# Scan layer of a four-layer network on one core: softplus by ScalarE's own function, three of sixteen products on GpSimd, x added by TensorE, rows issued by SyncE

## The chip, the core and the metric

The kernel runs on one core of a Trainium2 chip. The time is that of one execution on the device, in microseconds. The median of three runs of the kernel before was 3129.49 us (3125.74 to 3132.32). Five engines work side by side, each through its own list of instructions in the written order: TensorE (PE in the profile, its weight loads PEld), VectorE (DVE), ScalarE (ACT), GpSimd (POOL) and SyncE (SP), which here only issues DMAs. They wait for each other through semaphores. SBUF is the working memory of 128 partitions; PSUM is the one TensorE writes to.

## What is computed

Three triangle layers come first and aren't touched. The fourth is a selective scan (Mamba) over the image: 256 columns, each a sequence of 256 rows with 32 channels, group-normalised first, and added to x at the end.

```python
xz = xs @ W_in; xi, z = jnp.split(xz, 2, axis=-1)            # 64 + 64
xc = silu(causal_conv(xi, conv_w) + conv_b)                   # 4 taps
dt_r, Bc, Cc = jnp.split(xc @ W_x, [dtr, dtr + d_state], -1)  # 2, 16, 16
dt = softplus(dt_r @ W_dt + b_dt)
A = -jnp.exp(A_log)
def step(h, inp):
    x_t, dt_t, B_t, C_t = inp
    h = jnp.exp(dt_t[:, :, None] * A) * h + dt_t[:, :, None] * B_t[:, None, :] * x_t[:, :, None]
    return (h, jnp.einsum('bds,bs->bd', h, C_t))
y = (scan(step, h0, ...) + xc * D_skip) * silu(z)
x = x + y @ W_out
```

All arithmetic is float32.

## The kernel before

`mamba_layer` cuts the 256 columns into four groups of 64 that lie on different partitions, and each group into 32 chunks of two columns (SUB). A chunk thus holds eight sequences of 256 rows; they are processed as two halves q of four sequences each along the 1024 free elements (W; HALF is 512) and 64 channels on two blocks of partitions. A state tile has 16 states x 8 channels on its 128 partitions, so a chunk has 16 **steps** s: eight groups of channels (dg) for each half q. In a step:

- SP loads the rows of dt for this group from DRAM, spread over the states, into `dtb` (ring of 4, 512 KB, L541).
- ACT makes the decays exp(dt*A) from `dtb` into `da` (ring of 4, L399). It does so one step ahead: in step s it makes those of s+1.
- PE spreads dt*x over the states into the PSUM tile `pb[s % 2]` (L282), waiting until scan s-2 has released it.
- DVE multiplies `pb` by B in place (L472), then scans with `da` and `pb` into `hs` (ring of 4, L477).
- POOL multiplies `hs` by C (L500).
- PE sums over the states into `py` (L265), for step s-3 (LAG). At dg 0 it starts the sum with D_skip*x (L261).

Beside its steps each engine has shares of the preparation of the next chunk (PRE), of its own chunk (OWN), of the one after next (NEXT2) and of the chunk before (POST). The table `SHARES` gives for each engine the step after which a share stands; function `schedule` writes step, shares, next step, share... in that order for each engine. Nothing moves later: this written order is what each engine follows. The shares: xg (normalised input, ACT L321), x (convolution, PE L230, four matmuls, silu L334), z (PE L236, silu L343), dt (PE L241, softplus on ACT and POOL), bq and cq (B and C of a half, PE L249, copied by ACT L391), take (y from PSUM, ACT L309), gate (times silu z, POOL L506), out (PE L293), its sum with x into `fin` (DVE L484), the stores of fin (ACT L416) and the rows of dt to DRAM (ACT L357). The softplus is built as max(v, 0) + ln(1 + exp(-|v|)) with a correction of the rounding of 1 + u: six ACT operations of full width (L364 to L383) and, on POOL, six operations of half width (L517, L520, L524), then dt*x in two halves (L527).

x, dt, z, bq and cq pass through the same two PSUM banks `misc[0..1]`. The table `USE` fixes their turn in a chunk; each writer on PE waits until ACT has emptied the bank of the one before. Before, that turn is x, bq1, cq1, dt, z, bq0, cq0. The chunks 1 to 28 run in a hardware loop of 14 rounds of two.

Of the kernel before, what the change touches and what calls it, by code (L numbers as in the profile page):

```python
# [5 lines left out]
P = 128  # L6
# [3 lines left out]
ALU = mybir.AluOpType  # L10
# [3 lines left out]
def mamba_layer(nc, shared, dt_dram, out):  # L14
# [15 lines left out]
    LAG = 3  # L30

    with ExitStack() as ctx:
# [11 lines left out]
        minus_one = sb("minus_one", [P, 1])  # L44
# [5 lines left out]
        (avg, w_in, conv_w, w_z, wx_dt, w_dt, w_bc, w_out, w_skip, vecs, a_log, spread, gather) = (t for t, _ in shared.weights)  # L50
# [16 lines left out]
        hs = sb("hs", [P, H_RING, W])  # L67
        gated = sb("gated", [P, W])
# [12 lines left out]
        with nc.Block() as block:  # L81
# [23 lines left out]
            def _(v):  # L105
                nc.vector.memset(minus_one[:, :], -1.0)
# [34 lines left out]
        def early(k, n):  # L141
            return isinstance(k, int) and k < n

        FIRST_USE = {"x": 0, "dt": 1, "z": 2, "bq0": 3, "cq0": 4}
        USE = {"x": 0, "bq1": 1, "cq1": 2, "dt": 3, "z": 4, "bq0": 5, "cq0": 6}

        def use(k, name):
            if early(k, 1) and name in FIRST_USE:
                return FIRST_USE[name]
            body = k if name in ("bq1", "cq1") else k - 1  # L150
            if isinstance(k, int) and body == CHUNKS - 1:
                return len(FIRST_USE) + len(USE) * body + ("bq1", "cq1").index(name)
            return len(FIRST_USE) + len(USE) * body + USE[name]

        def stores_of(k, par):
# [62 lines left out]
        with nc.Block() as block:  # L218
            @block.tensor
            def _(pe):  # L220
                def pre(k, par, op):
# [47 lines left out]
                def steps(k, par, s, first, last):  # L269
# [1365 lines left out]
```

## Time and profile before

| | |
|---|---|
| median of three runs | 3129.49 us |
| span of the profiled execution | 3123.6 us |
| scan layer, first scan to end of last | 1295.6 to 3110.6 us |
| busy over the whole span: PE, DVE, ACT, POOL | 82%, 80%, 61%, 66% |

The profile is of one execution. Its busy shares over the whole span mix the triangle layers (until about 1240 us) with the scan layer; for the change the rows of the second half count. Rows of a timeline give start and duration in us, the engine, the line of the kernel, the operation, output and inputs with their sizes, the count of merged instructions and, in brackets, the idle time of the engine before them with what ended it. A matmul in float32 leaves two records, so x8 stands for four matmuls.

### The profile page before, as it was taken

To read this page: it belongs to the slowest core of one execution; us is meant where nothing else is said; L and a number is where in the kernel's file an instruction comes from. 1 tells how busy PE (TensorE), PEld (TensorE's weight loads), DVE (VectorE), ACT (ScalarE), POOL (GpSimd) and SP (SyncE) were. 2 spreads that over 40 slices of the span, in tenths; PEclk is the share of its full clock that TensorE was granted. 3 is DMA by queue.
4 is the path that set the end of the run, shared out by engine and by line. 5 is a ranking of instruction groups with operands and counts; after the bars stand their busy time and mean duration, and the time that the engine had idled before them with its cause. 6 is when DMAs were issued, how large, how long until landed. Compare 5 with 4: busy or idle time off the path is not lost.

```text
span 3123.6 us, 40760 instructions
## 1 busy us (share of the span) xinstructions
PE 2573.1 (82%) x12954; PEld 756.1 (24%) x12954; DVE 2485.6 (80%) x2176; ACT 1914.4 (61%) x2402; POOL 2065.3 (66%) x1284
## 2 busy tenths in 40 slices
PE   5888878888788775688888888888888888888886
PEld 1233123331233211222222222222222222222221
DVE  5655656555555544599999999999999999999998
ACT  4534654346543343667777777677777776777772
POOL 2543245432444313298898888988988889889886
PEclk9999999999999988799999999999999999999999
DMA  4797327863279647667677677676775766767765
GB/s 162 241 325 212 102 67 255 294 205 102 72 241 313 192 133 181 132 146 181 147 165 167 144 177 163 148 181 148 162 170 145 179 160 148 180 148 162 171 145 117
DMA packets 257701, 537.53 MB, mean 172 GB/s; under 512 B 39608, under 2 KB 150656, under 8 KB 256688
## 3 DMA queue, kind: packets, MB, share of 16 engines
q1 hardware_dynamic: 215328, 444.01, 53.7%
q0 software_dynamic: 19040, 64.24, 7.7%
q10 hardware_dynamic: 23216, 27.74, 3.7%
q8 instruction: 71, 1.16, 0.2%
q14 instruction: 46, 0.38, 0.0%
HBM read 396.55 MB, written 139.33 MB: 172 GB/s over the span
## 4 chain that ended last, share of the span: by engine, by line
POOL 29%; issue 27%; PE 5%; DVE 2%; DMA 2%; ACT 1%; SPq 1%; POOLq 0%; ACTq 0%; DVEq 0%
POOL m_hs L500 18%; POOL m_sp_v L517 2%; POOL m_dtx L527 2%; POOL m_gated L506 2%; DMA t_tile<-band_out 1%; POOL m_dt L524 1%; POOL m_dt L520 1%; SPq L913 1%; DVE m_pb L472 1%; PE t_bank L1096 1%; PE t_bank L1057 1%; PE t_bank L1021 1%; POOL t_xc L1481 1%; DVE m_hs L477 1%; PE m_misc L230 0%
## 5 line engine op out<-in xcount | busy, mean ns | idle before, releaser
L500 POOL TENSOR_TENSOR m_hs<-m_hs,m_cs 128x1024 f32<-128x1024 f32 x512 | 1203.6, 2358 | 288.4 <-DVE m_hs L477 288.4
L477 DVE TENSOR_TENSOR_SCAN m_hs<-m_da,m_pb 128x1024 f32<-128x1024 f32 x512 | 1170.7, 2287 | 29.3 <-ACT m_da L399 4.2
L399 ACT ACTIVATE m_da<-m_dtb,m_a_neg 128x1020 f32<-128x1020 f32 x512 | 576.6, 1144 | 275.9 <-DMA m_dtb<-dt_rows 254.1
L282 PE MATMUL m_pb<-m_dtx,late 64*128 64x512 f32 x2048 | 583.5, 646 | 150.2 <-DVE m_hs L477 146.9
L265 PE MATMUL m_py<-m_hs,late 128*64 128x512 f32 x2048 | 565.8, 631 | 104.8 <-POOL m_hs L500 104.0
L472 DVE TENSOR_TENSOR m_pb<-m_pb,m_bs 128x1024 f32<-128x1024 f32 x512 | 619.7, 1210 | 20.9 <-PE m_pb L282 20.9
L1481 POOL TENSOR_TENSOR t_xc<-t_xc,big 128x512 f32<-128x512 f32 x96 | 120.1, 1271 | 338.8 <-DVE big L1387 338.8
L282 PEld LDWEIGHTS m_pb<-m_dtx,late 64*128 64x128 f32 x2048 | 163.4, 188 | 567.3 <-DVE m_hs L477 457.5
L1021 PE MATMUL t_bank<-late,t_lwin 128*128 128x256 f32 x816 | 217.3, 404 | 63.3 <-ACT big L1260 34.0
L1359 DVE SCALAR_TENSOR_TENSOR t_xc<-t_bank,t_vec,t_xc 128x512 f32<-128x512 f32 x96 | 72.0, 750 | 244.2 <-PE t_bank L1057 244.2
L1248 ACT ACTIVATE t_sq<-t_bank 128x512 f32<-128x512 f32 x192 | 105.5, 598 | 245.3 <-PE t_bank L1096 245.2
L1257 ACT ACTIVATE t_gate<-t_bank,t_small 128x512 f32<-128x512 f32 x192 | 121.4, 683 | 191.0 <-PE t_bank L1031 190.9
L265 PEld LDWEIGHTS m_py<-m_hs,late 128*64 128x64 f32 x2048 | 102.5, 136 | 509.3 <-POOL m_hs L500 279.6
L1478 POOL TENSOR_TENSOR t_sq<-big 128x512 f32<-128x512 f32 x96 | 103.1, 1082 | 185.2 <-ACT big L1230 112.2
L1377 DVE SCALAR_TENSOR_TENSOR t_tile<-t_bank,t_small,t_gate 128x512 f32<-128x512 f32 x192 | 135.2, 746 | 89.6 <-issue 59.4
L1344 DVE TENSOR_TENSOR t_vwin<-t_bank,t_mask_k 128x512 f32<-128x512 f32 x204 | 138.0, 687 | 83.9 <-PE t_bank L1021 64.8
L1413 POOL DMA_DIRECT2D late<-right_factor x96 | 56.9, 593 | 212.6 <-PE t_bank L1021 156.4
L1021 PEld LDWEIGHTS t_bank<-late,t_lwin 128*128 128x128 f32 x816 | 146.6, 193 | 175.3 <-issue 83.3
L1096 PE MATMUL t_bank<-t_tile,t_center 64*64 64x512 f32 x768 | 125.8, 668 | 68.8 <-DMA t_tile<-band_out 54.6
L391 ACT COPY m_cs<-m_misc 128x512 f32<-128x512 f32 x128 | 68.7, 589 | 154.1 <-PE m_misc L249 154.1
L321 ACT ACTIVATE m_xg<-big,m_gn_bias,m_gn_scale 64x512 f32 (+1 forms) x126 | 161.2, 1279 | 1.7
L249 PE MATMUL m_misc<-m_act,late 64*128 64x512 f32 x512 | 147.1, 651 | 13.6 <-ACT m_act L343 11.1
(166 smaller groups left out, 3591.3 us busy)
## 6 DMA issues: line engine op xcount, KB each, us to landing
m_dtb<-dt_rows SPq DMA_DIRECT2D x512, 512.0 KB, 6.1
late<-right_factor POOLq DMA_DIRECT2D x102, 512.0 KB, 5.5
right_factor<-t_tile SPq DMA_DIRECT2D x192, 256.0 KB, 3.5
t_tile<-band_out SPq DMA_DIRECT2D x183, 256.0 KB, 4.2
band_out<-t_vwin SPq DMA_DIRECT2D x48, 512.0 KB
band_out<-t_vwin SPq DMA_DIRECT2D x48, 480.0 KB
dt_rows<-m_dt ACTq DMA_DIRECT2D x64, 256.0 KB, 3.2
t_xc<-in_x_cm SPq DMA_DIRECT2D x4, 2048.0 KB, 14.6
```

What stands on the lines that cost most here:

```text
L249: nc.tensor.matmul(misc[n][:, :], w_bc[rows, b, :], act[par][rows, half(q)], start=True, stop=True).then_inc(misc_ready[n], 1)
L265: m = nc.tensor.matmul(py[q][D * n:D * n + D, :], gather[:, dg, :], hs[:, s % H_RING, half(n)], start=False, stop=(dg == DG - 1), skip_gro ...
L282: m = nc.tensor.matmul(pb[s % 2][:, half(n)], spread[rows, dg, :], dtx[par][rows, half(q)], start=True, stop=True)
L321: m = nc.scalar.activation(xg[par][P // 4 * shift:P // 4 * shift + P // 2, q, :, first:first + T], xm[rows, :, bass.ds(SUB * k, SUB)].rear ...
L399: nc.scalar.activation(da[:, s % DA_RING, :, 1:T], dtb[s % DTB_RING][:, :].rearrange("p (r t) -> p r t", t=T)[:, :, 1:T], ACT.Exp, scale=a ...
L472: nc.vector.tensor_tensor(pb[s % 2][:, :], pb[s % 2][:, :], bs[q][:, :], ALU.mult).then_inc(u_done, 1)
L477: nc.vector.tensor_tensor_scan(hs[:, s % H_RING, :], da[:, s % DA_RING, :, :].rearrange("p r t -> p (r t)"), pb[s % 2][:, :], 0.0, ALU.mul ...
L500: nc.gpsimd.tensor_tensor(hs[:, s % H_RING, :], hs[:, s % H_RING, :], cs[q][:, :], ALU.mult).then_inc(hc_ready, 1)
L1021: m = nc.tensor.matmul(bank[b][:, e * COLS:(e + 1) * COLS], lwin[:, slot, LROW * h + BAND:LROW * h + BAND + P], rwin[:, slot, h * COLS:(h ...
L1096: m = nc.tensor.matmul(bank[p][o:o + HID, :], center64[HID * hs:HID * hs + HID, HID * hs:HID * hs + HID], tile[HID * hs:HID * hs + HID, sl ...
L1344: nc.vector.tensor_tensor(vwin[:, slot, UNIT * j:UNIT * j + UNIT].rearrange("p (h k) -> p h k", k=COLS), bank[b][:, :].rearrange("p (h k) ...
L1481: nc.gpsimd.tensor_tensor(x_unit(n), x_unit(n), xn_unit(n), ALU.add).then_inc(x_done, 1)
```

## The change

- **Softplus.** One ACT activation per half (Softplus with bias) from `misc` to `dt`. The six ACT operations and the six on POOL are gone. Silus of x and z stand together at step 6; the table is loaded for silu, back, for softplus at step 8, back.
- **Products.** For s in POOL_U (5, 10, 15) PE spreads dt*x into `misc` instead of `pb` (shares u5, u10, u15, at steps 0, 4, 10), ACT copies it to `ub` (ring of 2), POOL multiplies it by B. The decays of these steps go to the PSUM tile `pb[s % 2]`, which has no product in that step. ACT first writes the zeros of its first columns, and waits for scan s-2 instead of s-4.
- **Turn of misc.** u5, bq1, cq1, u10, x, z, dt, bq0, u15, cq0. On PE x and z both stand after step 5.
- **x** is added by a matmul of an identity (`eye`, a new weight) with x, read with a step of a row, into py[1] ahead of out; ACT copies the sum to `fin` at step 9.
- **SP** issues the rows of dt (step 13) and the stores of fin (step 14).
- The loop of 14 rounds is written out.

```diff
+    POOL_U = (5, 10, 15)
+    UB_RING = 2
...
-        USE = {"x": 0, "bq1": 1, "cq1": 2, "dt": 3, "z": 4, "bq0": 5, "cq0": 6}
+        FIRST_USE = {op: i for i, op in enumerate(("x", "z", "dt", "bq0", "cq0"))}
+        USE = {op: i for i, op in enumerate(("u5", "bq1", "cq1", "u10", "x", "z", "dt", "bq0", "u15", "cq0"))}
...
-            "tensor": {0: [(PRE, "x")], 2: [(OWN, "bq1")], 4: [(OWN, "cq1")], 5: [(PRE, "dt")],
-                       8: [(PRE, "z"), (POST, "out")], 9: [(PRE, "bq0")], 11: [(PRE, "cq0")]},
...
+            "tensor": {0: [(OWN, "u5")], 1: [(OWN, "bq1")], 3: [(OWN, "cq1")], 4: [(OWN, "u10")], 5: [(PRE, "x"), (PRE, "z")],
+                       7: [(PRE, "dt")], 8: [(POST, "out")], 9: [(PRE, "bq0")], 10: [(OWN, "u15")], 11: [(PRE, "cq0")]},
+            "scalar": {1: [(OWN, "u5")], 2: [(OWN, "bq1")], 4: [(POST, "take1"), (OWN, "cq1")], 5: [(OWN, "u10")], 6: [(PRE, "silu")],
+                       8: [(PRE, "dt")], 9: [(POST, "fin")], 10: [(PRE, "bq0")], 11: [(OWN, "u15")], 12: [(PRE, "cq0"), (OWN, "take0")],
+                       13: [(NEXT2, "xg0")], 15: [(NEXT2, "xg1")]},
+            "vector": {},
+            "gpsimd": {1: [(OWN, "u5")], 5: [(POST, "gate1")], 6: [(OWN, "u10")], 9: [(PRE, "dtx0")], 10: [(PRE, "dtx1")], 11: [(OWN, "u15")],
+                       13: [(OWN, "gate0")]},
+            "sync": {13: [(PRE, "dt_rows")], 14: [(POST, "store")]},
...
-            with eng.Fori(1, CHUNKS - 4, 2) as k:
-                chunk(k, 1, (NEXT2, PRE, OWN, POST))
-                chunk(k + 1, 0, (NEXT2, PRE, OWN, POST))
-            chunk(CHUNKS - 3, 1, (NEXT2, PRE, OWN, POST))
+            for k in range(1, CHUNKS - 2):
+                chunk(k, k % 2, (NEXT2, PRE, OWN, POST))
...
+                    elif op[0] == "u":
+                        q, dg = divmod(int(op[1:]), DG)
+                        pe.wait_ge(dtx_ready, 2 * k + q + 1)
+                        for n in range(2):
+                            pe.wait_ge(misc_used[n], use(k, op))
+                        for n in range(2):
+                            rows = slice(D * n, D * n + D)
+                            nc.tensor.matmul(misc[n][:, :], spread[rows, dg, :], dtx[par][rows, half(q)],
+                                             start=True, stop=True).then_inc(misc_ready[n], 1)
...
-                    if not (first and s < 2):
-                        pe.wait_ge(h_ready, g - 1)
...
+                    if s not in POOL_U:
+                        if not (first and s < 2):
+                            pe.wait_ge(h_ready, g - 1)
...
+                    nc.tensor.matmul(py[1][:, :], eye[:, :], xm[:, :, SUB * k:SUB * k + SUB].rearrange("p t n -> p n t"),
+                                     start=True, stop=False, skip_group_check=True)
...
+                    elif op == "dt":
+                        a.preload_act_table_set("softplus")
...
+                            nc.scalar.activation(dt[:, half(q)], misc[q][:, :], ACT.Softplus, bias=b_dt).then_inc(misc_used[q], 1)
+                        a.preload_act_table_set("natural_log_exp_and_others")
...
+                    if s in POOL_U:
+                        a.wait_ge(h_ready, g - 1)
+                        to = pb[s % 2][:, :].rearrange("p (r t) -> p r t", t=T)
+                        nc.scalar.copy(to[:, :, 0:1], zeros[:, :].unsqueeze(2))
+                    else:
+                        if not (first and s < DA_RING):
+                            a.wait_ge(h_ready, g - DA_RING + 1)
+                        to = da[:, s % DA_RING, :, :]
+                    nc.scalar.activation(to[:, :, 1:T], rows, ACT.Exp, scale=a_neg[:, dg:dg + 1]).then_inc(da_ready, 1)
...
+                    a.wait_ge(o_ready, k + 1)
+                    if not early(k, 1):
+                        a.wait_ge(stored, 16 * G * k)
+                    nc.scalar.copy(fin[:, :], py[1][:, :]).then_inc(fin_done, 1)
...
+                    decays, products = da[:, s % DA_RING, :, :].rearrange("p r t -> p (r t)"), pb[s % 2][:, :]
+                    if s in POOL_U:
+                        j = pool_products(k, s)
+                        v.wait_ge(ub_ready, j + 1)
+                        decays, products = pb[s % 2][:, :], ub[j % UB_RING][:, :]
```

## Rows read from the trace of the kernel before

**Rows 1.** The page, part 1: busy us, share of the span, instructions.
```profile
PE 2573.1 (82%) x12954; PEld 756.1 (24%) x12954; DVE 2485.6 (80%) x2176; ACT 1914.4 (61%) x2402; POOL 2065.3 (66%) x1284
```

**Rows 2.** First to last scan: length; busy PE, PEld, DVE, ACT, POOL; clock; DMA share; GB/s.
```profile
1295.60:3110.60 1815.00, 1558.73 (x5334) 410.89 (x5332) 1778.87 (x1054) 1317.53 (x1442) 1577.46 (x822) 0.99 0.69 160
```

**Rows 3.** Groups by line, 1400 to 3110 us: busy us, mean ns | idle before, releaser.
```profile
L500 POOL TENSOR_TENSOR m_hs<-m_hs,m_cs 128x1024 f32<-128x1024 f32 x483 | 1135.3, 2358 | 214.9 <-DVE m_hs L477 214.9
L477 DVE TENSOR_TENSOR_SCAN m_hs<-m_da,m_pb 128x1024 f32<-128x1024 f32 x483 | 1104.4, 2287 | 23.8
L472 DVE TENSOR_TENSOR m_pb<-m_pb,m_bs 128x1024 f32<-128x1024 f32 x482 | 583.4, 1210 | 10.0 <-PE m_pb L282 10.0
...
L321 ACT ACTIVATE m_xg<-big,m_gn_bias,m_gn_scale 64x512 f32 x110 | 140.7, 1279 | 1.5
...
L520 POOL TENSOR_TENSOR m_dt<-m_dt,m_sp_v 128x512 f32<-128x512 f32 x58 | 74.2, 1279 | 2.3
...
L334 ACT ACTIVATE m_act<-m_misc,late 128x512 f32<-128x512 f32 x58 | 36.7, 684 | 0.3
...
L484 DVE TENSOR_TENSOR m_fin<-m_py,big 128x512 f32<-128x512 f32 x30 | 31.2, 1039 | 0.0
L364 ACT ACTIVATE m_sp_u<-m_sp_x 128x1024 f32<-128x1024 f32 x29 | 30.7, 1057 | 2.3
```

**Rows 4.** Waits of DVE, 1400 to 3100 us: us in total, times, longest us.
```profile
DVE m_pb L472 <- PE m_pb L282: 10.0, 29, 0.6
```

**Rows 5.** Timeline of DVE in one chunk.
```profile
2263.31 1.23 DVE L472 TENSOR_TENSOR m_pb<-m_pb,m_bs 128x1024 f32<-128x1024 f32 x1 [0.48 <-PE m_pb L282]
...
2278.54 2.29 DVE L477 TENSOR_TENSOR_SCAN m_hs<-m_da,m_pb 128x1024 f32<-128x1024 f32 x1
2280.74 1.21 DVE L472 TENSOR_TENSOR m_pb<-m_pb,m_bs 128x1024 f32<-128x1024 f32 x1
2281.98 2.29 DVE L477 TENSOR_TENSOR_SCAN m_hs<-m_da,m_pb 128x1024 f32<-128x1024 f32 x1
```

**Rows 6.** Timeline of PE in the same chunk.
```profile
2258.21 3.99 PE L230 MATMUL m_misc<-m_xg,m_w_conv 128*128 128x512 f32 x8
2262.14 1.13 PE L282 MATMUL m_pb<-m_dtx,late 64*128 64x512 f32 x4
2263.20 1.08 PE L265 MATMUL m_py<-m_hs,late 128*64 128x512 f32 x4
...
2286.39 1.98 PE L236 MATMUL m_misc<-m_xg,late 64*128 64x512 f32 x4
2288.30 1.08 PE L293 MATMUL m_py<-m_gated,late 128*64 128x512 f32 x4
```

**Rows 7.** Timeline of ACT in the same chunk.
```profile
2262.39 1.28 ACT L328 ACT_TABLE_LOAD   x1
...
2268.36 1.05 ACT L391 COPY m_bs<-m_misc 128x512 f32<-128x512 f32 x2
2269.30 1.15 ACT L399 ACTIVATE m_da<-m_dtb,m_a_neg 128x1020 f32<-128x1020 f32 x1
2270.34 0.58 ACT L309 COPY m_gated<-m_py 128x512 f32<-128x512 f32 x1
```

**Rows 8.** Groups by line of ACT, whole program: a tiny operation.
```profile
L91 ACT ACTIVATE m_gn_scale<-m_gn_scale 128x1 f32<-128x1 f32 x1 | 0.2, 203 | 0.0
```

**Rows 9.** Timeline of PE at the end of the chunk.
```profile
2302.53 1.13 PE L282 MATMUL m_pb<-m_dtx,late 64*128 64x512 f32 x4 [1.31 <-DVE m_hs L477]
2304.77 1.98 PE L265 MATMUL m_py<-m_hs,late 128*64 128x512 f32 x4 [1.11 <-POOL m_hs L500]
```

**Rows 10.** Stretches of 2 us, columns as in Rows 2: chunk before, this chunk.
```profile
2246.00:2248.00 2.00, 0.88 (x6) 0.18 (x4) 1.97 (x2) 1.97 (x2) 2.00 (x2) 1.00 0.41 98
...
2309.00:2311.00 2.00, 2.00 (x6) 0.42 (x4) 1.97 (x3) 0.00 (x0) 2.00 (x2) 0.51 0.57 176
```

**Rows 11.** Timeline: the first scan.
```profile
1295.61 2.29 DVE L477 TENSOR_TENSOR_SCAN m_hs<-m_da,m_pb 128x1024 f32<-128x1024 f32 x1 [4.21 <-ACT m_da L399]
```

More of the change, by code:

```diff
@@ L67, in mamba_layer @@
         hs = sb("hs", [P, H_RING, W])
+        ub = [sb(f"ub{i}", [P, W]) for i in range(UB_RING)]
+        zeros = sb("zeros", [P, 2 * SUB])
         gated = sb("gated", [P, W])
@@ L141, in early @@
         def early(k, n):
-            return isinstance(k, int) and k < n
-        FIRST_USE = {"x": 0, "dt": 1, "z": 2, "bq0": 3, "cq0": 4}
-        USE = {"x": 0, "bq1": 1, "cq1": 2, "dt": 3, "z": 4, "bq0": 5, "cq0": 6}
+            return k < n
+        FIRST_USE = {op: i for i, op in enumerate(("x", "z", "dt", "bq0", "cq0"))}
+        USE = {op: i for i, op in enumerate(("u5", "bq1", "cq1", "u10", "x", "z", "dt", "bq0", "u15", "cq0"))}
+        OWN_USE = ("u5", "bq1", "cq1", "u10", "u15")
         def use(k, name):
@@ L149, in use, with dve_products, pool_products @@
                 return FIRST_USE[name]
-            body = k if name in ("bq1", "cq1") else k - 1
-            if isinstance(k, int) and body == CHUNKS - 1:
-                return len(FIRST_USE) + len(USE) * body + ("bq1", "cq1").index(name)
+            body = k if name in OWN_USE else k - 1
+            if body == CHUNKS - 1:
+                return len(FIRST_USE) + len(USE) * body + OWN_USE.index(name)
             return len(FIRST_USE) + len(USE) * body + USE[name]
+        def dve_products(k, s):
+            return (S - len(POOL_U)) * k + s - sum(t < s for t in POOL_U)
+        def pool_products(k, s):
+            return len(POOL_U) * k + sum(t < s for t in POOL_U)
         def stores_of(k, par):
@@ L180, in schedule @@
-        def schedule(eng, name, pre, steps, post):
+        FIRST = {"vector": {9: [(PRE, "dtx0"), (PRE, "dtx1")]}, "gpsimd": {}}
+        def schedule(name, pre, steps, post):
             def share(k, par, kinds, s):
-                table = FIRST if kinds == (PRE,) and k == -1 and name in FIRST else FIRST_X if isinstance(k, int) and k == -2 and name in FIRST_X else SHARES
+                table = FIRST if kinds == (PRE,) and k == -1 and name in FIRST else FIRST_X if k == -2 and name in FIRST_X else SHARES
@@ L413, in post @@
                         return take(k, par, 1)
-                    a.wait_ge(fin_done, k + 1)
-                    for g in range(G):
-                        a.dma_start(out[:, bass.ds(SUB * k + g * NG, SUB), :],
-                                    fin[DM * g:DM * g + DM, :].rearrange("p (n t) -> p n t", n=SUB)).then_inc(stored, 16)
-                schedule(a, "scalar", pre, steps, post)
+                    a.wait_ge(o_ready, k + 1)
+                    if not early(k, 1):
+                        a.wait_ge(stored, 16 * G * k)
+                    nc.scalar.copy(fin[:, :], py[1][:, :]).then_inc(fin_done, 1)
+                schedule("scalar", pre, steps, post)
             @block.vector
@@ L476, in steps @@
                         v.wait_ge(hc_used, g - H_RING + 1)
[L477 to L489 removed]
+                    nc.vector.tensor_tensor_scan(hs[:, s % H_RING, :], decays, products, 0.0, ALU.mult, ALU.add).then_inc(h_ready, 1)
+                schedule("vector", pre, steps, None)
             @block.gpsimd
@@ L537, in steps @@
                         sp.wait_ge(dt_stored[par], stores_of(k, par))
-                    elif not (first and s < DTB_RING):
+                    if not (first and s < DTB_RING):
                         sp.wait_ge(da_ready, g - DTB_RING + 1)
@@ L543, in steps, with pre, post @@
                                  ).then_inc(dtb_loaded[s % DTB_RING], 16)
-                schedule(sp, "sync", None, steps, None)
+                def pre(k, par, op):
+                    for q in range(2):
+                        sp.wait_ge(misc_used[q], use(k, "dt") + 1)
+                    if not early(k, 2):
+                        sp.wait_ge(da_ready, S * (k - 1))
+                    for n in range(2):
+                        sp.dma_start(dt_dram[par, :, :, n, :].rearrange("q d c -> d q c"),
+                                     dt[D * n:D * n + D, :].rearrange("d (q c) -> d q c", q=2)).then_inc(dt_stored[par], 16)
+                def post(k, par, op):
+                    sp.wait_ge(fin_done, k + 1)
+                    for g in range(G):
+                        sp.dma_start(out[:, SUB * k + g * NG:SUB * k + g * NG + SUB, :],
+                                     fin[DM * g:DM * g + DM, :].rearrange("p (n t) -> p n t", n=SUB)).then_inc(stored, 16)
+                schedule("sync", pre, steps, post)
                 sp.wait_ge(stored, 16 * G * CHUNKS)
```

201 lines of the change are left out of this document (57 added, 144 removed).

## Prediction

> **What bounds the kernel now.** Read the page's busy shares first [rows 1]: over the whole program no engine is full, but the scan layer is the second half, and there the stretch view is the one to read. Between the first and the last scan, 1815 us, DVE is busy 1778.9 us, 98%, PE 86%, POOL 87%, ACT 73% [rows 2]. That is 32 chunks of 56.7 us. The groups by line say what DVE does in a chunk [rows 3]: 16 scans of 2.29 us and 16 products (L472) of 1.21 us, 56.0 us, and one addition of x (L484) of 1.04 us; neighbours overlap by some 0.05 to 0.09 us. DVE's waits hold one line, the product L472 waiting for PE, 10.0 us in 30 chunks [rows 4]. The timelines show where that is: step to step is 3.45 us [rows 5], except once a chunk, 0.5 us late, because the next matmul of L282 stands in PE's queue behind the x matmuls (3.9 us) [rows 5, 6]. So DVE is the bound, but PE, which works in the written order, has only that much room behind it.
>
> **Work removed and added, per chunk.** On DVE three of 16 products go, and the addition of x. A step whose product comes from elsewhere is a scan alone: 2.2 us from start to start, the distance from a scan to what follows it [rows 5]. 13 x 3.45 + 3 x 2.2 = 51.4 us against 56.7. The scan still reads one operand from PSUM and one from SBUF, only exchanged, so I keep 2.29 us (nothing in the trace has the exchanged form; it could be 0.1 us either way, 0.3 a chunk).
> On POOL six half-width operations of the softplus go (6 x 1.28 = 7.7 us), three products of full width come (3 x 2.36 = 7.1) [rows 3]: 87% of 56.7 is 49.3, now 48.7 us. It fits under 51.4, barely. The products are due three to four steps after they are issued, so POOL delays nothing.
> On ACT six full-width operations of some 1.06 us go [rows 3]; six copies of 0.58, the copy of fin (0.6) and three zero columns (a tiny ACT operation takes 0.20 us [rows 8]) come: 41.2 - 6.4 + 4.7 = 39.5 us. The table loads stay four (before: two pairs around the silus; now silu, exp, softplus, exp) at 1.28 us each [rows 7]. Hidden, as long as ACT is not on a chain; below it is.
> On PE the three spread matmuls only change their target; the identity matmul for x is new. A 128-row matmul of 512 columns takes 1.0 us (a quarter of the 3.9 for x, half of the 1.9 for z [rows 6]). Its moving operand is read with a step of a whole row. The nearest rows for such a read are ACT's L321 at 1.28 us against L334 at 0.68 for a contiguous one [rows 3], a factor of 1.9; so I take 1.9 us, bounds 1.0 and 2.5 (both records of the matmul at 1.28). PE needs about 50 us of a chunk: it too only just fits under 51.4.
> The Trainium skill (SBUF — State Buffer, Door 1) says that SBUF is read in lines of 16 bytes and that each access in a new line pays; that speaks against this matmul. It agrees in direction with L321; by the page alone no figure follows, and with contiguous reads the sum would be unchanged, since the 0.6 us of lateness this gives to product 9 lies beside another one (below).
> The rows of dt leave on SP instead of ACT, at step 13, behind load 13 and ahead of load 14. They no longer wait for POOL's fix-up; SP's loads of the next chunk come earlier. The four stores of fin go to SP too, behind load 14; what queues behind them is loads 15 and on, which run four decays ahead. ACT's long waits for these loads cost DVE nothing before, so I price the move at 0 (bounds -0.5 and +0.5 us a chunk, a load issued late by the 0.6 us or so of each of the six issues).
> The loop of 14 rounds is written out. DVE shows no wait at its ends [rows 4], so nothing is gained there: 0.
>
> **What the new order does.** misc[0..1] now has ten users a chunk in strict turn: u5, bq1, cq1, u10, x, z, dt, bq0, u15, cq0. In PE's written order z has moved up beside x, so between the spread matmul of step 4 and that of step 6 stand: sums 1 and 2, u10, x and z. Step 5 has no spread matmul of its own, so DVE asks for that of step 6 a scan earlier than the pace of the steps suggests. Count from the end of scan 3, t=0. DVE's own path: product 4 at -0.1, scan 4 at 1.15, scan 5 at 3.35, product 6 due at 5.55.
> The supply: the decay of step 5 is written to the PSUM bank that scan 3 read, so ACT waits there until t=0, and the take of y and the copies of cq1 stand behind it on ACT. u10 may write misc only after those copies; PE, in order, waits with everything behind it. Zero column 0.2, decay 1.05, take 0.5, copies 1.1 [rows 7, 8], with 0.1 for the wait: 2.9. u10 1.05 (as the spread matmul L282), sum 2 1.0 [rows 6]: 5.0. x 3.9: 8.9. z 1.9: 10.8 (the silus of x end at 8.3 and 9.7, in time for it, table load included). Spread matmul 6 to product 6 1.2 [rows 5, 6]: **12.0**. Product 6 is 6.5 us late in every chunk that prepares a next one. Even with no wait at all for ACT, PE has 7.0 us between these two matmuls and is given about 9.1 of work, so over 2 us would remain.
> A second, smaller chain of the same kind: decay 10 waits for scan 8; behind it fin 0.5, decay 11 1.05, copies of bq0 1.1, u15 1.1, spread matmul 11 1.2: product 11 starts 6.3 after scan 8 instead of 5.55, 0.7 late. The lateness of product 9 from the identity matmul lies inside it.
> **The clock.** PE idles before u10, from about t=-1.3 (sum 1 done) to 2.9. What a gap does to it is in the trace: at the end of a chunk, after idle times of 1.3 and 1.1 us around one matmul group, the granted clock fell from 1.00 to 0.50 (1.2 GHz) until about 2311, the sums then taking 1.97 us instead of 1.08; in the chunk before, the same pattern passed at 1.00 [rows 9, 10]. A gap of 4.2 us is larger than these, so I expect the half clock under u10 and the first x matmuls in nearly all chunks. The Trainium skill (TensorE: Matmul & The Clock Gate, What's actually happening) says that the low clock is the default and activity lifts it; the row agrees. Rows show low stretches that cost from 0 up to 3.1 us (half of 6.2); I take 1.7, about the middle. Near the chunk's end two more gaps (waits for POOL at sum 12 and for scan 14) can do the same; the matmuls there have about a step of room, so 0.5 (0 to 1.5).
>
> **The sum.** Chunk: 51.4 + 6.5 + 0.7 + 1.7 + 0.5 = 60.8 us against 56.7, +4.1. Thirty-one chunks prepare a next one: +127. The last has no x and z: 51.4 + 0.7, -4.6. Ahead of the first scan (1295.6 [rows 11]) the softplus chain of three ACT and nine DVE pieces goes and z comes in: -6 (-8 to 0). At the end fin is 0.4 shorter, the identity matmul adds up to 2 at the low clock: +1.5. Together +118. Profiled execution 3123.6 -> 3242; the median of the runs stands 5.9 higher, 3129.5 -> **3247 us**. Low end: clock terms 0, chain 0.5 shorter: 58.1 a chunk, 31 x 1.4 - 9 = +34, 3163. High end: 3.1 + 1.5 for the clock, 0.6 more for the identity matmul: 63.8, 31 x 7.1 - 9 = +211, about 3340.
>
> **The rivals.**
> A. *DVE stays the bound*: no lateness at products 6 and 11, 51.9 us a chunk with small waits: -154 -5, about 2970, clearly faster. For it: each engine's work fits, POOL and PE under 51.4. Against: it needs spread matmul 6 to start by t=4.4, that is x and z out of the way before; with DVE's pace given, PE would have to take later matmuls first. What decides is PE's order. That it keeps it the trace shows: the spread matmul at 2262.14 stood ready behind x while DVE waited [rows 5, 6]. The Trainium skill (TensorE: Matmul & The Clock Gate, Step-by-step: what each phase is for) says that matmuls stay in program order and only weight loads are pulled ahead; by that rule this rival falls.
> B. *Only PE's load counts*: ACT frees misc earlier than I hold (the wait for scan 3 ends early), product 6 about 2.6 late: 51.4 + 2.6 + 0.7, -2.0 a chunk, about 3060. Against: the wait is written ahead of the copies on ACT, and nothing lets ACT pass it.
> C. *The strided matmul is dear*, 4 us rather than 1.9: product 9 becomes 2.7 late, +2.0 on each chunk on top of the forecast: about 3310.
> D. *The added and the saved cancel*: chain 3 us shorter and the clock held: within 0.2%.
>
> **How the numbers follow.** Forecast (lateness at product 6 of 5 us or more) 0.69; C 0.08; A 0.13; B 0.07; D 0.03. Slower 0.77, same 0.03, faster 0.20 (0.2%, 6 us, is about what can be told from no change). The range has to reach from the forecast's low end, with something for a shorter chain, to C: 3145 to 3335; A and B stay out of it.
>
> **What would show it.** Timeline of DVE: product 6 starts some 12 us after scan 3 ends, not 5.6, and DVE's waits name PE at L472 with about 200 us or more; DVE's share falls from 98% to about 85%. Timeline of PE: idle before u10 until the copies of cq1, then x and z back to back, the clock near 0.5 at its start. ACT idle before decay 5 until scan 3. If product 6 is in time, the chain is wrong; if the x matmuls run at 1.00, the clock term is; if the identity matmul takes 1.0 us, its price was too high, with no effect on the sum.

## The result and the profile after

The changed kernel takes 3252.55 us, the median of 4 runs (3238.95 to 3266.88), against 3129.97 (3125.74 to 3132.32, also 4) for the kernel before on the same chip: ratio 1.0385, interval 1.0345 to 1.0425. It is slower by 3.9%. The profiled execution spans 3242.0 us, against 3123.6.

First the page: busy time, and the slices of DVE and of PE's clock.

```profile
PE 2700.6 (83%) x13018; PEld 808.9 (25%) x13018; DVE 2342.8 (72%) x2039; ACT 1859.9 (57%) x2534; POOL 2053.0 (63%) x1194
...
DVE  5655656556554442878888888888888889788787
...
PEclk9999999999989887899899998999998999898998
```

In [rows 1] DVE was busy 80% of the span; now it has 143 us less work and the span is 118 us longer. In the scan layer no engine is full any more. This is the stretch 1400 to 3000 us (columns as in [rows 2]); DVE is at 85%, where [rows 2] had 98%:

```profile
1400.00:3000.00 1600.00, 1398.66 (x4518) 384.93 (x4514) 1365.97 (x772) 1065.03 (x1322) 1306.03 (x613) 0.92 0.61 153
```

The waits from 1400 to 3220 us name what DVE, PE and ACT stand still for (total, times, longest). This answers [rows 4], where DVE waited 10.0 us in all:

```profile
DVE m_pb L450 <- PE m_pb L290: 255.1, 137, 9.0
...
PE m_misc L243 <- ACT m_cs L380: 104.2, 30, 3.7
PE m_py L272 <- POOL m_hs L468: 77.7, 30, 2.6
...
ACT m_pb L390 <- DVE m_hs L455: 388.4, 90, 10.0
```

L450 is now DVE's product, L455 the scan, L290 the spread matmul, L243 the matmul of a product for POOL, L272 the sum over states, L468 POOL's product with C, L380 the copies of B and C, L390 the zero column ahead of a decay in PSUM. The first, second and last of these lines, read upwards, make a circle: ACT waits for a scan, PE for ACT's copies, DVE for PE.

One chunk as DVE sees it (the place of [rows 5]): scans 3, 4 and 5, then product 6 after 5.89 us of idling, and products 9 and 12.

```profile
2334.35 2.29 DVE L455 TENSOR_TENSOR_SCAN m_hs<-m_da,m_pb 128x1024 f32<-128x1024 f32 x1
...
2337.80 2.29 DVE L455 TENSOR_TENSOR_SCAN m_hs<-m_da,m_pb 128x1024 f32<-128x1024 f32 x1
2340.00 2.27 DVE L455 TENSOR_TENSOR_SCAN m_hs<-m_pb,m_ub 128x1024 f32<-128x1024 f32 x1
2348.16 1.23 DVE L450 TENSOR_TENSOR m_pb<-m_pb,m_bs 128x1024 f32<-128x1024 f32 x1 [5.89 <-PE m_pb L290]
...
2359.18 1.23 DVE L450 TENSOR_TENSOR m_pb<-m_pb,m_bs 128x1024 f32<-128x1024 f32 x1 [0.57 <-PE m_pb L290]
...
2368.58 1.23 DVE L450 TENSOR_TENSOR m_pb<-m_pb,m_bs 128x1024 f32<-128x1024 f32 x1 [0.23 <-PE m_pb L290]
```

The same microseconds on ACT and PE (the places of [rows 7] and [rows 6]):

```profile
2336.73 0.17 ACT L390 COPY m_pb<-m_zeros 128x4 f32<-128x4 f32 x1 [6.29 <-DVE m_hs L455]
2336.83 1.11 ACT L395 ACTIVATE m_pb<-m_dtb,m_a_neg 128x1020 f32<-128x1020 f32 x1
2337.88 0.58 ACT L319 COPY m_gated<-m_py 128x512 f32<-128x512 f32 x1
2338.36 1.07 ACT L380 COPY m_cs<-m_misc 128x512 f32<-128x512 f32 x2
```

```profile
2339.57 1.13 PE L243 MATMUL m_misc<-m_dtx,late 64*128 64x512 f32 x4 [3.43 <-ACT m_cs L380]
2340.63 1.08 PE L272 MATMUL m_py<-m_hs,late 128*64 128x512 f32 x4
2341.64 3.70 PE L228 MATMUL m_misc<-m_xg,m_w_conv 128*128 128x512 f32 x8
2345.27 1.55 PE L234 MATMUL m_misc<-m_xg,late 64*128 64x512 f32 x3
...
2346.77 1.33 PE L290 MATMUL m_pb<-m_dtx,late 64*128 64x512 f32 x3
...
2355.10 1.96 PE L300 MATMUL m_py<-big,late 128*128 128x512 f32 x2
```

Scan 3 ends at 2336.64, and ACT's zero column starts 0.09 us later. Decay, take and copies run to 2339.43, u10, sum 2, x and z to 2347.25, the first of the four spread matmuls of step 6 among those of z. Product 6 starts 11.5 us after the scan. Here the clock was at 1.00 throughout. In other chunks it fell: PE was idle from 2394.7 to 2398.2, then sum 2 took 1.85 us instead of 1.08 and x 4.58 instead of 3.70. Stretches of 2 us, clock in the third column from the right:

```profile
2398.00:2400.00 2.00, 1.80 (x6) 0.53 (x8) 2.00 (x2) 1.71 (x4) 1.20 (x1) 0.86 0.92 219
2400.00:2402.00 2.00, 2.00 (x5) 0.50 (x2) 0.90 (x1) 1.98 (x3) 2.00 (x2) 0.50 0.90 225
2402.00:2404.00 2.00, 2.00 (x5) 0.90 (x4) 0.00 (x0) 0.81 (x1) 2.00 (x2) 0.79 0.86 174
```

### The profile page after: what moved, and what is told of

It reads as the page before. It is cut to its first block, busy times and chain, and to the rows that moved or that the text cites. A ratio compares the mean times of both kernels' runs of the same rounds, so it can differ in the third digit from the quotient of the medians.

```text
span 3242.0 us, 37780 instructions
## 1 busy us (share of the span) xinstructions
PE 2700.6 (83%) x13018; PEld 808.9 (25%) x13018; DVE 2342.8 (72%) x2039; ACT 1859.9 (57%) x2534; POOL 2053.0 (63%) x1194
## 3 DMA queue, kind: packets, MB, share of 16 engines
q1 hardware_dynamic: 230832, 469.25, 52.1%
## 4 chain that ended last, share of the span: by engine, by line
DVE 23%; PE 21%; issue 11%; ACT 5%; POOL 1%; DVEq 0%; ACTq 0%; POOLq 0%
DVE m_hs L455 12%; DVE m_pb L450 11%; PE m_pb L290 5%; PE m_misc L228 4%; PE m_py L272 4%; PE m_misc L243 3%; PE m_misc L234 2%; PE m_misc L256 1%; PE m_py L268 1%; ACT m_bs L380 1%; ACT m_cs L380 1%; ACT m_da L395 1%; ACT m_gated L319 1%; ACT m_fin L411 1%; POOL m_hs L468 0%
## 5 line engine op out<-in xcount | busy, mean ns | idle before, releaser
L468 POOL TENSOR_TENSOR m_hs<-m_hs,m_cs 128x1024 f32<-128x1024 f32 x512 | 1199.2, 2353 | 414.2 <-DVE m_hs L455 410.9
L455 DVE TENSOR_TENSOR_SCAN m_hs<-m_da,m_pb 128x1024 f32<-128x1024 f32 x416 | 951.2, 2286 | 19.3 <-ACT m_da L395 4.9
L450 DVE TENSOR_TENSOR m_pb<-m_pb,m_bs 128x1024 f32<-128x1024 f32 x416 | 505.8, 1216 | 279.4 <-PE m_pb L290 279.4
L272 PE MATMUL m_py<-m_hs,late 128*64 128x512 f32 x2048 | 613.1, 680 | 85.2 <-POOL m_hs L468 85.2
L290 PE MATMUL m_pb<-m_dtx,late 64*128 64x512 f32 x1664 | 509.3, 660 | 42.8 <-DVE m_hs L455 42.8
L395 ACT ACTIVATE m_da<-m_dtb,m_a_neg 128x1020 f32<-128x1020 f32 x416 | 472.2, 1150 | 2.1
L390 ACT COPY m_pb<-m_zeros 128x4 f32<-128x4 f32 x96 | 15.8, 165 | 419.8 <-DVE m_hs L455 419.8
L290 PEld LDWEIGHTS m_pb<-m_dtx,late 64*128 64x128 f32 x1664 | 161.3, 197 | 332.3 <-issue 249.0
L272 PEld LDWEIGHTS m_py<-m_hs,late 128*64 128x64 f32 x2048 | 107.5, 143 | 511.1 <-issue 311.1
L243 PE MATMUL m_misc<-m_dtx,late 64*128 64x512 f32 x384 | 125.0, 726 | 124.5 <-ACT m_cs L380 111.1
L484 POOL TENSOR_TENSOR m_ub<-m_ub,m_bs 128x1024 f32<-128x1024 f32 x96 | 226.1, 2356 | 0.0
L455 DVE TENSOR_TENSOR_SCAN m_hs<-m_pb,m_ub 128x1024 f32<-128x1024 f32 x96 | 217.3, 2264 | 0.0
```

What stands on the lines that cost most here:

```text
L243: nc.tensor.matmul(misc[n][:, :], spread[rows, dg, :], dtx[par][rows, half(q)], start=True, stop=True).then_inc(misc_ready[n], 1)
L272: m = nc.tensor.matmul(py[q][D * n:D * n + D, :], gather[:, dg, :], hs[:, s % H_RING, half(n)], start=False, stop=(dg == DG - 1), skip_gro ...
L290: m = nc.tensor.matmul(pb[s % 2][:, half(n)], spread[rows, dg, :], dtx[par][rows, half(q)], start=True, stop=True)
L395: nc.scalar.activation(to[:, :, 1:T], rows, ACT.Exp, scale=a_neg[:, dg:dg + 1]).then_inc(da_ready, 1)
L450: nc.vector.tensor_tensor(products, products, bs[q][:, :], ALU.mult).then_inc(u_done, 1)
L455: nc.vector.tensor_tensor_scan(hs[:, s % H_RING, :], decays, products, 0.0, ALU.mult, ALU.add).then_inc(h_ready, 1)
```

## The experiments

Times are medians; ratios are to the kernel before on the same chip. A chunk is the distance between the first scans of neighbouring chunks, its mean over the 31 chunks that have a next one (from the timelines of DVE). It belongs to the one execution that was profiled; for "z a step later" that was the slowest of the four (3259.5 us, the others 3226.3 to 3233.6), so its 61.2 is too long for the median beside it. The kernels ran on several chips, so the ratios compare better than the medians.

| kernel | us | ratio, interval | chunk, us |
|---|---|---|---|
| before | 3129.97 | | 56.8 |
| after | 3252.55 | 1.0385, 1.0345 to 1.0425 | 60.5 |
| z a step later | 3230.6 | 1.0315, 1.0266 to 1.0365 | 61.2 |
| decays in SBUF | 3159.9 | 1.0066, 1.0034 to 1.0098 | 57.9 |
| copies ahead of the pinned decay | 3120.6 | 0.9953, 0.9931 to 0.9975 | 56.7 |
| PE's gap filled | 3199.1 | 1.0199, 1.0170 to 1.0227 | 59.2 |
| x read contiguously | 3233.7 | 1.0306, 1.0276 to 1.0337 | 60.5 |
| no products on POOL | 3163.3 | 1.0066, 1.0029 to 1.0102 | 57.7 |
| the same, z at step 7 | 3145.7 | 1.0030, 1.0015 to 1.0045 | 57.5 |
| the same, steps 7 to 10 spread | 3107.8 | 0.9917, 0.9896 to 0.9939 | 56.3 |
| PE reordered, x on DVE | 3052.3 | 0.9732, 0.9704 to 0.9759 | 54.5 |
| PE reordered, x on PE | 3053.3 | 0.9732, 0.9716 to 0.9749 | 54.5 |
| reordered, clock kept, x on DVE | 2987.2 | 0.9516, 0.9496 to 0.9536 | 52.4 |
| reordered, clock kept, x on PE | 2977.5 | 0.9506, 0.9482 to 0.9529 | 52.1 |

**Is it z alone?**

```
-  5: [(PRE, "x"), (PRE, "z")],
+  5: [(PRE, "x")], 6: [(PRE, "z")],
```

> The changed kernel with z moved on PE from behind x (step 5) to behind step 6; all else stays. Theory (PE works through a block without a pause from u10 to the spread matmul of step 9, so only the total in that block and the pause ahead of it count): the wait of product 6 falls by 1.9 us, from 5.9 to 8.4 down to about 4 to 6.5, products 7 to 9 become late instead (about 0.5, 0.5 and 1.5 us), and the time stays within 0.3% of the changed kernel, 3240 to 3260 us. Rival (the place of z at step 5 is what costs): 31 x 1.9 = 59 us less, about 3190 us.

Waits of DVE in one chunk:

```profile
2237.99 1.23 DVE L450 TENSOR_TENSOR m_pb<-m_pb,m_bs 128x1024 f32<-128x1024 f32 x1 [7.22 <-PE m_pb L290]
2241.77 1.23 DVE L450 TENSOR_TENSOR m_pb<-m_pb,m_bs 128x1024 f32<-128x1024 f32 x1 [0.23 <-PE m_pb L290]
2245.85 1.23 DVE L450 TENSOR_TENSOR m_pb<-m_pb,m_bs 128x1024 f32<-128x1024 f32 x1 [0.52 <-PE m_pb L290]
2250.72 1.23 DVE L450 TENSOR_TENSOR m_pb<-m_pb,m_bs 128x1024 f32<-128x1024 f32 x1 [1.32 <-PE m_pb L290]
```

Product 6 still waits 5.6 to 7.4 us, and what z gave back is asked for again at products 7 to 9. PE was late as a whole; taking one block out of one gap only passes the lateness on. The time is that of after or up to 1% less, 3230.6 us where 3240 to 3260 was expected; the rival asked for 3190.

**Is it the pinned decay?** First without it: the decays of 5, 10 and 15 go to the SBUF ring like the others.

```
-  if s in POOL_U:
-      a.wait_ge(h_ready, g - 1)
-      to = pb[s % 2][:, :].rearrange("p (r t) -> p r t", t=T)
-      nc.scalar.copy(to[:, :, 0:1], zeros[:, :].unsqueeze(2))
-  else:
   if not (first and s < DA_RING):
       a.wait_ge(h_ready, g - DA_RING + 1)
   to = da[:, s % DA_RING, :, :]
...
-  decays, products = pb[s % 2][:, :], ub[j % UB_RING][:, :]
+  products = ub[j % UB_RING][:, :]
```

> The changed kernel with the decays of steps 5, 10 and 15 in the SBUF ring like all others, waiting for the scan four steps back; no zero columns. Theory (the pin of ACT on the scan two steps back, ahead of the copies of cq1, delays u10): ACT copies cq1 early, product 6 waits about 2.6 us instead of 5.9 to 8.4, PE has no long pause before u10 and keeps its clock: 55 us a chunk instead of 60.3, about 3090 us. Rival 1 (ACT is not the cause, only the amount of work on PE): product 6 waits 6 us or more and the time stays near 3250. Rival 2 (a scan with both operands in SBUF is slower, by POOL's use of SBUF for instance): mean of these 96 scans above 2.35 us.

The wait of product 6 fell to 3.12 us (2.6 expected):

```profile
2303.97 1.23 DVE L445 TENSOR_TENSOR m_pb<-m_pb,m_bs 128x1024 f32<-128x1024 f32 x1 [3.12 <-PE m_pb L290]
```

The theory of the pin holds, but the time missed, 3159.9 us where 3090 was expected, and the chunk fell only to 57.9. Here rival 2 came true as well: the 91 scans with both operands in SBUF took 2.92 us on average (1400 to 3150 us) where 2.35 was its mark, since they collide with POOL. At three such scans a chunk that is 1.9 us. Scans and POOL's operations of one stretch:

```profile
2318.74 2.27 DVE L450 TENSOR_TENSOR_SCAN m_hs<-m_da,m_ub 128x1024 f32<-128x1024 f32 x1
...
2335.17 4.18 DVE L450 TENSOR_TENSOR_SCAN m_hs<-m_da,m_ub 128x1024 f32<-128x1024 f32 x1
```

```profile
2318.90 4.26 POOL L463 TENSOR_TENSOR m_hs<-m_hs,m_cs 128x1024 f32<-128x1024 f32 x1 [1.95 <-DVE m_hs L450]
...
2332.55 4.66 POOL L463 TENSOR_TENSOR m_hs<-m_hs,m_cs 128x1024 f32<-128x1024 f32 x2
2337.17 3.24 POOL L469 TENSOR_TENSOR m_gated<-m_gated,m_act 128x512 f32<-128x512 f32 x1
```

The scan that began first (2318.74) took its 2.27 us, and POOL's operation, begun 0.16 later, 4.26 instead of 2.35: 1.91 longer, where 2.1 of the scan were left. The scan at 2335.17 met a running POOL operation that ended at 2337.21 and took 4.18; the gate that began then took 3.24 instead of 1.27. Each waits out the other whole. In after, with one operand in PSUM, no scan is long: 91 with a mean of 2.264 us. The Trainium skill (SBUF — State Buffer, Who interferes with whom) says that a VectorE instruction with two inputs in SBUF and a GpSimd one that reads SBUF exclude each other for a whole instruction, and that the first to start wins; these rows agree, with the four durations above. So placing those decays in PSUM has a purpose: it costs ACT the pin and saves the scans this.

Then with the pin, but the copies no longer behind it:

```
 tensor  -  3: cq1, 4: u10, 5: x, z         +  2: cq1, 3: u10, 5: x, z
 scalar  -  4: take1, cq1, 5: u10           +  3: cq1, u10, 4: take1
```

> The changed kernel with cq1 and u10 each a step earlier on PE and both copied ahead of the pinned decay 5 on ACT; decays in PSUM, x and z behind step 5 as in the changed kernel. Theory (the pin is in the chain, and what is left is the amount of work between two spread matmuls): product 6 waits about 2.6 us instead of 5.9 to 8.4, no low clock in front of x: 55.1 us a chunk, about 3085 us. Rival 1 (the pin doesn't matter): product 6 still 6 us or more late, 3240 us. Rival 2 (x and z together don't matter once the pin is out of the way): under 1 us, about 3040 us.

```profile
2221.79 1.55 PE L234 MATMUL m_misc<-m_xg,late 64*128 64x512 f32 x3 [1.02 <-ACT m_act L343]
```

Product 6 waits 3.21 us in nearly every chunk instead of 5.89 to 8.40 (the row below), PE no longer idles before u10, and 132 us are gone (3252.6 to 3120.6): slower has become slightly faster. The run moves two things together: the copies ahead of the pin, and u10, 1.0 us, out of the block between spread matmuls 4 and 6. What each brings, and what comes from the clock, isn't separated by it; the run before moves the pin alone, but pays with long scans. The time is 35 us more than expected: x now ends so early that z waits 1.02 for the silu of x (the line above), and product 1 waits 0.76 to 1.38 us in 18 of the 31 chunks behind the pauses at the chunk's end, with matmuls at twice their time there.

```profile
2224.68 1.23 DVE L450 TENSOR_TENSOR m_pb<-m_pb,m_bs 128x1024 f32<-128x1024 f32 x1 [3.21 <-PE m_pb L290]
```

**Is the clock a cost of its own?** Three matmuls with zero weights (zw), added to a bank already being summed, before u10:

```
+  if op == "u10":
+      for _ in range(3):
+          nc.tensor.matmul(py[0][:, :], zw[:, :], act[par][:, half(0)], start=False, stop=False,
+                           skip_group_check=True)
```

> The changed kernel with three matmuls of a zero weight (128 rows, 512 columns, adding nothing) on PE ahead of the wait of u10: 3 us of work more per chunk in a pause of about 4.2 us. Theory (the pause lowers the granted clock in two chunks of three): waits of product 6 all near 5.9 us instead of 5.9, 7.5, 8.4, the time 31 x 1.4 = 43 us less, about 3210 us. Rival (the three values come from something else, DMA for instance): no gain, or up to 30 us more for the work added, 3250 to 3280 us.

With work added, the time fell by 53 us (43 expected). Product 6 waits 5.89 to 6.17 in all chunks that prepare a next one, but for the first (5.40), and the mean clock rose from 0.924 to 0.942. The mean of its three waits in after is (5.89 + 7.54 + 8.40) / 3 = 7.28 us, so the clock cost about 1.4 us a chunk there; the chunks agree, 60.5 against 59.2.

**The strided read.** Here other elements of x are added, read contiguously:

```
-  xm[:, :, SUB * k:SUB * k + SUB].rearrange("p t n -> p n t")
+  shared.big[:, HALF * k:HALF * k + HALF]
```

> The changed kernel with the identity matmul reading 512 elements in a row instead of 512 with a step of a row; it adds other elements of x than the reference. Theory: the matmul takes 1.0 us instead of 1.96; the 0.6 us of wait at product 9 goes and comes back at product 11 through the chain decay 10, fin, decay 11, bq0, u15; the time stays within 0.3% of the changed kernel, 3240 to 3260 us. Rival (each us of PE counts one for one): 31 x 0.9 = 28 us less, about 3225 us.

Groups of after and of this kernel:

```profile
L300 PE MATMUL m_py<-big,late 128*128 128x512 f32 x60 | 58.8, 1069 | 0.0
```

```profile
L300 PE MATMUL m_py<-big,late 128*128 128x512 f32 x60 | 33.8, 645 | 0.0
```

The stride costs 0.42 us on each of two records. Product 9's wait of 0.57 went, 0.35 came at product 11 and product 12 waited 0.44 instead of 0.23, and the chunk stayed at 60.5: no term of the sum. The median is 19 us lower all the same, a little below the 3240 expected; of the 10.7 us between the two profiled spans 8.0 lie ahead of the first scan and 2.5 in the chunks.

**Softplus, fin and SP alone.** `POOL_U = ()`, and u5, u10, u15 out of all tables (a); then z moved (b); then the blocks spread, fin at step 10 with them (c). PE's steps:

```
 (a)  5: x, z   7: dt    8: out         9: bq0
 (b)  5: x      7: z     8: dt, out     9: bq0
 (c)  5: x      7: z     8: dt          9: out        10: bq0
```

> The changed kernel with all 16 products on DVE and all decays in SBUF; softplus, fin by identity matmul, SP's rows and the order with x and z behind step 5 stay. Theory (x and z back to back, 5.8 us between two spread matmuls, are late even without a pinned decay): product 6 waits about 2.3 us, a chunk takes 55.2 + 2.3 + 0.5 = 58 us, about 3165 us. Rival (the pin alone makes the lateness): product 6 waits 0.5 us or less, 55.7 us a chunk, 3090 us.

> As e7_no_products, with z behind step 7 and dt behind step 8. Theory: no wait of DVE over 0.6 us, 55.6 us a chunk, so what the softplus, fin on PE and SP's rows bring by themselves: 32 x 1.1 + 6, about 3090 us. Rival (the new parts have a cost of their own besides the order): 3120 us or more.

> As e8_no_products_z7, with out and the identity matmul a step later (9), bq0 behind step 10 and fin on ACT at step 10, so that no block of over 3 us but x stands between two spread matmuls. Theory (e8's wait of 2.1 us a chunk came from dt, identity and out standing together behind step 8): waits of DVE under 0.6 us a chunk, 55.8 us a chunk, 3129.5 - 32 x 0.9 - 6 = about 3095 us, the gain of softplus and fin without the products. Rival (something else in the new parts costs): 3130 us or more.

Waits of DVE in (a), (b), (c), 1400 to 3000 us:

```profile
DVE m_pb L449 <- PE m_pb L290: 64.6, 55, 1.8
```

```profile
DVE m_pb L449 <- PE m_pb L290: 59.0, 28, 2.1
```

```profile
DVE m_pb L449 <- PE m_pb L290: 25.5, 28, 0.9
```

In (a) z behind x costs 1.76 us at product 6 (2.3 expected), and the time came out as expected, 3163 us. (b) was expected to run in 3090 us and took 3145.7; it removed the wait of product 6 and put one of 2.11 at product 9: my own order set dt, the identity matmul and out between two spread matmuls, 1.8 + 1.8 + 1.0 us. In (c) 0.91 us remains, at product 10, and the parts of the change without the products bring 0.8%, 3107.8 us where 3095 was expected. In the profiled execution 8.9 of the 22.5 us gained lie ahead of the first scan; per chunk it is 56.3 against 56.8. What counts is how much PE is given between two spread matmuls, not how much in a chunk.

**All of the change, in another order on PE.**

```
 tensor  0: u5  1: bq1  2: cq1  3: u10  4: x   7: z   8: dt   9: out  10: u15  11: bq0  13: cq0
 scalar  1: u5  2: bq1  3: cq1, u10   4: take1   6: silu   8: dt   10: (fin,) u15   11: bq0
         12: take0   13: cq0
```

u15 also takes `misc` ahead of bq0.

> The changed kernel in another order: cq1 and u10 each a step earlier on PE and ahead of the pinned decay 5 on ACT, x behind step 4, z alone behind step 7, dt behind 8, u15 ahead of bq0, cq0 behind 13; x is added by DVE again (step 9) and the identity matmul is out. Theory (the order on PE, not the parts of the change, costs the time): PE finds its work when its banks are free, product 6 waits under 1 us, a chunk takes 52.4 to 54 us, 3129.5 - 32 x 3.5 - 5: about 3010 us (2990 to 3040). Rival (PE and POOL at 95% of a chunk can't be kept fed: gaps and the low clock take the gain): 56 us or more a chunk, 3100 us or more.

> The same order with the identity matmul for x on PE and fin on ACT as in the changed kernel. Theory: PE has 2 us more to do and DVE 1 us less; PE is the fuller engine, so a chunk takes about 1 us more than in e5_reordered_dve_x, 3040 us. Rival (DVE is the bound in this order): 1 us less a chunk, about 2985 us.

Both bring 2.7%. That is less than expected (3010 and 3040 us, 52.4 to 54 us a chunk), and whether DVE or PE adds x makes no difference. In the version with x on DVE small waits remain, 1.34 us at product 1 and 0.47 at product 6 the largest. PE at the chunk's end shows why:

```profile
2217.64 1.08 PE L272 MATMUL m_py<-m_hs,late 128*64 128x512 f32 x4 [1.99 <-POOL m_hs L472]
2220.50 2.08 PE L290 MATMUL m_pb<-m_dtx,late 64*128 64x512 f32 x4 [1.78 <-DVE m_hs L450]
2222.51 1.97 PE L272 MATMUL m_py<-m_hs,late 128*64 128x512 f32 x4
```

After idle times of 1.99 and 1.78 us around one sum every matmul takes twice its time, the pattern of [rows 9]. A zero matmul on either side of that sum tests it:

```
+  if s == S - 1:
+      nc.tensor.matmul(py[1][:, :], zw[:, :], act[par][:, half(1)], start=False, stop=False,
+                       skip_group_check=True)
   sum_states(k, par, s - LAG)
+  if s == S - 1:
+      nc.tensor.matmul(py[1][:, :], zw[:, :], act[par][:, half(1)], start=False, stop=False,
+                       skip_group_check=True)
```

> The order of e5_reordered_dve_x, with one matmul of a zero weight (adding nothing) on either side of sum 12 in step 15 on PE, where it waits 2.0 us for POOL and 1.8 us for scan 14. Theory (this pause lowers the clock, and the slow matmuls behind it make product 1 of the next chunk 1.34 us late): that wait goes, 31 x 1.3 = 40 us less than 3052, about 3012 us. Rival (the wait at product 1 comes from the order alone, and the added 2 us of PE work count): 3050 us or more.

> e6_reordered (x added by the identity matmul on PE, fin copied by ACT) with the same two zero matmuls around sum 12 as e9_keep_clock. In e9_keep_clock DVE is busy 99% of a chunk of 52.4 us and never waits for PE. Theory (DVE is the bound there): the 0.95 us of DVE saved would bring 30 us, but PE then needs 49 + 2 = 51 us and its order leaves no room, so DVE waits for it about 1 us a chunk: the same time as e9_keep_clock, 2975 to 3005 us. Rival 1 (PE keeps up): 2957 us. Rival 2 (the identity matmul costs its full 2 us on a full PE): 3020 us or more.

Stretch 1400 to 2900 us, x on DVE, without and with the two matmuls:

```profile
1400.00:2900.00 1500.00, 1366.84 (x4618) 394.76 (x4614) 1433.04 (x824) 1091.84 (x1346) 1350.12 (x632) 0.94 0.68 169
```

```profile
1400.00:2900.00 1500.00, 1407.41 (x4933) 403.95 (x4934) 1487.08 (x861) 1135.47 (x1405) 1407.94 (x660) 1.00 0.72 175
```

The clock is at 1.00 and DVE at 99%: it is the bound again, with the shorter list of work that the change gave it. 3012 us was expected with x on DVE, the wait at product 1 gone; 2987.2 came, since that at product 6 went too. With x on PE the chunk is 52.1 us and the whole 2977.5 us (2975 to 3005 expected), 4.9% under the kernel before. The two intervals overlap.

## Why the prediction was right, and where it was not

**The answer.** 3247 us was forecast and 3252.6 measured, slower, inside 3145 to 3335.

**What bounds.** Right: DVE is the bound, "but PE, which works in the written order, has only that much room behind it". The 5.3 us a chunk taken off DVE were nearly all real: in the best version DVE's chunk is 52.1 us with 0.4 of waits, so 51.7, where the sum had 51.4. The exchanged operands cost nothing (2.264 us against 2.286).

**The chain of product 6.** Each step stands in the trace above: zero column 0.17 (0.2 forecast), decay 1.11 (1.05), take and copies as forecast. The copies ended 2.8 us after scan 3 (2.9), product 6 started 11.5 after it (12.0). Its wait was 5.89 us where the clock held (6.5). The size that was most off is x: 3.63 us from start to start, not 3.9. PE's pause ahead of u10 was 3.43 us where 4.2 was forecast, as sum 1 ended 0.5 us before scan 3 did and not 1.3. The pin's part is shown by the decays in SBUF, where only the pin goes: 3.12 us. That something stays without it is shown by the same wait, and by 3.21 with the copies ahead of the pin; the prediction had "over 2 us", from 9.1 us of work, where its own sizes add up to 8.85. The run without products doesn't test this figure, since u10 is gone there too; its 1.76 us is what x and z alone leave.

**The clock.** 1.7 us a chunk forecast at u10 and x; 1.4 measured, by the filled gap and by the mean of three chunks alike. But "in nearly all chunks" was wrong: it fell in two of three. The waits go 5.89, 7.54, 8.40 in turn, and the chunks are 59.0, 60.3 and 61.6 us long.

**The rest of the chunk.** Product 9 waited 0.57 and product 12 0.23, together 0.80 where 0.7 was forecast for product 11 with that of 9 inside it. Product 11 started 6.2 us after scan 8 (6.3 forecast) and didn't wait, since product 9 had already put DVE back; the wait at product 12 wasn't foreseen. Products 0 and 1 waited 0.18 and 0.26 on average (0.5 forecast). The identity matmul took 1.96 us (1.9). Over the 31 chunks product 6 waited 7.4 us on average, the last few longer than the three values above; forecast were 6.5 + 1.7 = 8.2. What is left of the chunk for DVE's own work is 51.9 us, 0.5 more than the sum had. Part of that is that a product which waits no longer overlaps the scan before it (2.29 us long, 2.20 to the next start). So the chunk is 51.9 + 7.4 + 0.8 + 0.4 = 60.5 us, 60.8 forecast: a wait put too long and DVE's work put too short partly cancel.

**The rest of the span: misses that cancel.** Forecast: -6 before the first scan. From the start of the scan layer (its first operation on ACT) to the first scan it was 41.0 us before and 33.0 after, so -8.0; but the layer itself began 9.2 us later, 1263.8 against 1254.6. The first half is the same work in all kernels, and in the profiled runs of the 14 kernels the layer begins between 1253.7 and 1273.0: scatter, as I take it, that the sum had no term for; no kernel was profiled twice to show it. Now the tally: 31 x (60.53 - 56.77) = +116.4, last chunk 53.9 against 54.9, -1.0, prologue -8.0, first half +9.2, tail after the last scan 14.8 against 13.0, +1.8: together +118.4, and the spans differ by 118.4. The exact agreement of 3242 with the forecast is luck: the 31 chunks were put 10.7 us too dear (127 against 116.4), the last one 3.6 too cheap, and the late begin of the layer paid back the rest. The last chunk was put at 52.1 us; there product 6 waited 3.09 us without any x or z, since u10 and sum 2 behind PE's pause took 2.08 and 1.98 us, twice their time. With the gap filled it waited 0.54 there.

**The rivals.** A (DVE stays the bound) needed another order on PE, as the prediction put it; given that order and the clock, its time of 2970 came out as 2977. B (ACT frees misc early) is refuted by ACT's idling of 6.29 us. C (dear strided matmul) is refuted by 1.96 us. D (added and saved cancel) didn't come either, the chain being as long as forecast; its sum doesn't come out in the prediction: 60.8 - 3 - 2.2 = 55.6 us a chunk would be about 3086 us, 1.4% less, not within 0.2%. The range also ends at 3335, a little under the forecast's own high end of 3340.

**What stays open.** The move of rows and stores to SP was priced at 0 and never tried by itself; the run (c) holds it together with softplus and fin, so its own share is unknown. The same holds for the loop that is written out, in all kernels but the one before. Why the clock falls in two chunks of three and not in the third wasn't tried.

## What to carry over

When a bounding engine is relieved, look next at the largest block of work that the in-order engine behind it is given between two handovers; its mean load says little (PE was estimated at 50 us of 51.4 and made DVE wait over 8 us). A wait that is harmless to its own engine pins everything written behind it: put copies that others wait for ahead of it. Where an engine's clock falls after pauses, a few matmuls that add zero in the pauses can be worth more than they cost: here 65 us and 76 us between medians, about 2%.

## What the runs showed of the hardware, unexpected

A scan of 128x1024 fp32 with both operands in SBUF and a POOL operation exclude each other: 4.18 us instead of 2.28, and 4.26 instead of 2.35; with one operand in PSUM neither was slowed (means 2.264 and 2.353 us in after). A matmul of 512 fp32 columns read with a step of a row takes 1069 ns a record against 645. PE idling 3.5 us before u10 lowered the clock in some chunks (2398 us) and not in others (2339 us).
